# A fused attention and mixture-of-experts layer: work moved between VectorE and GpSimd, and a new order of the stage before attention

## What is computed

```python
xn = _layernorm(x, axis=-1)
queries, keys = xn @ w_q, xn @ w_k                    # 64 wide
scores = where(causal, queries @ keys.T * 64 ** -0.5, -inf)
attention = softmax(scores) @ (xn @ w_v1 @ w_v2)
logits = xn @ w_router.T                              # 16 experts
mask = one_hot(top_1(logits)); s = sigmoid(logits) * mask
gate, up = split((s.T[:, :, None] * xn) @ gate_up_proj)
expert_out = (up * silu(gate)) @ down_proj            # summed over experts
shared = (silu(xn @ w_gate.T) * (xn @ w_up.T)) @ w_down.T
moe = shared + expert_out
```

## Time and profile before

| | us |
|---|---|
| median of three runs | 242.66 (242.14 to 243.34) |
| the profiled execution | 243.21 |
| its span, first to last instruction | 239.9 |
| PE busy | 211.4 (88%) |
| PE weight loads busy | 183.3 (76%) |
| DVE busy | 155.7 (65%) |
| ACT busy | 130.6 (54%) |
| POOL busy | 110.8 (46%) |

### The profile page before, as it was taken

One profiled execution on the slowest core, in us unless ns is written; L12 is line 12 of the kernel. 1 busy time (PEld: TensorE's weight loads), 2 busy tenths in 40 slices (PEclk: granted clock), 3 DMA queues, 4 the chain that ended last, 5 costly groups with the idle time before them and its releaser, 6 DMA issues.

```text
span 239.9 us, 4858 instructions
## 1 busy us (share of the span) xinstructions
PE 211.4 (88%) x1399; PEld 183.3 (76%) x1401; DVE 155.7 (65%) x396; ACT 130.6 (54%) x329; POOL 110.8 (46%) x130
## 2 busy tenths in 40 slices
PE   4695999999996669999992899999999999899993
PEld 4484887898775559979881679998898897798792
DVE  3946887867748667678769466996665666405501
ACT  2354688678452566675674245554444444655741
POOL 1903030300001767777796006665665666738700
PEclk9997999999999999999998599999999999999999
DMA  6999999900000631541460113233233220019731
GB/s 174 398 361 337 190 172 303 256 23 0 0 4 1 176 99 55 146 132 48 103 172 0 47 44 87 78 85 80 85 84 87 81 77 19 3 45 290 237 87 44
DMA packets 30004, 28.26 MB, mean 118 GB/s; under 512 B 2563, under 2 KB 27146, under 8 KB 29344
## 3 DMA queue, kind: packets, MB, share of 16 engines
q1 hardware_dynamic: 27456, 23.77, 38.0%
q0 software_dynamic: 2528, 4.24, 5.6%
HBM read 14.28 MB, written 10.50 MB: 103 GB/s over the span
## 4 chain that ended last, share of the span: by engine, by line
PE 76%; DVE 12%; issue 5%; ACT 3%; DMA 1%; POOL 1%; DVEq 0%; ACTq 0%
PE acc L1163 13%; PE acc L1237 9%; PE big L1004 8%; PE big L1006 7%; PE big L1005 7%; PE mid L1147 6%; PE acc L1061 6%; PE mid L1226 4%; PE big L1134 4%; PE big L1131 4%; PE mid L1114 2%; DVE wel L732 2%; PE mid L1034 2%; PE acc L1025 1%; DVE stats L454 1%
## 5 line engine op out<-in xcount | busy, mean ns | idle before, releaser
L429 POOL DMA_INDIRECT y_rows<-y,ids x47 | 46.0, 978 | 36.7 <-ACT y L966 19.3
L419 POOL DMA_INDIRECT scratch<-rows,slot x32 | 32.3, 1009 | 41.3 <-DVE slot L651 30.7
L1163 PE MATMUL acc<-vr_all,pt 128*128 128x128 f32 x288 | 40.3, 277 | 0.6 <-ACT pt L912 0.3
L1163 PEld LDWEIGHTS acc<-vr_all,pt 128*128 128x128 f32 x288 | 36.5, 191 | 2.0 <-issue 1.1
L690 DVE TENSOR_REDUCE negmax<-big 128x1 f32<-128x128 f32 (+7 forms) x32 | 24.0, 755 | 21.2 <-PE big L1134 20.9
L905 ACT ACTIVATE prob<-big,negmax 128x128 f32<-128x128 f32 (+7 forms) x32 | 23.8, 744 | 19.6 <-DVE negmax L690 19.4
L912 ACT COPY pt<-mid 128x512 f32<-128x512 f32 (+3 forms) x48 | 22.8, 476 | 13.5 <-PE mid L1147 13.0
L774 DVE COPY eht<-mid 128x512 f32<-128x512 f32 (+1 forms) x24 | 16.3, 680 | 21.2 <-PE mid L1226 21.2
L966 ACT COPY y<-acc 128x256 f32<-128x256 f32 (+1 forms) x24 | 8.8, 368 | 34.0 <-PE acc L1237 34.0
L1237 PEld LDWEIGHTS acc<-wed,eht 128*128 128x128 f32 x188 | 24.5, 191 | 3.7 <-issue 1.9
L1147 PE MATMUL mid<-identf,prob 128*128 128x128 f32 x144 | 23.8, 274 | 3.3 <-ACT prob L905 2.7
(11 more groups left out here) (128 smaller groups left out, 439.2 us busy)
## 6 DMA issues: line engine op xcount, KB each, us to landing
we_raw<-w_gate_up SPq DMA_DIRECT2D x4, 1024.0 KB, 11.8
scratch<-blank SPq DMA_DIRECT2D x1, 3120.0 KB, 25.3
xe<-scratch SPq DMA_DIRECT2D x24, 130.0 KB
wed<-w_down SPq DMA_DIRECT2D x1, 2048.0 KB, 30.4
q_raw<-qk_all SPq DMA_DIRECT2D x8, 256.0 KB, 4.9
k_raw<-qk_all SPq DMA_DIRECT2D x8, 256.0 KB, 5.2
expert_out<-y_rows SPq DMA_DIRECT2D x8, 256.0 KB, 4.9
out<-res SPq DMA_DIRECT2D x8, 256.0 KB, 3.8
```

What stands on the lines that cost most here:

```text
L419: pool.indirect_dma_start(scratch, bass.IndirectOffsetOnAxis(ap=slot[:, t:t + 1], axis=0), rows[:, t, :], None).then_inc(row_sent[t % FLY] ...
L429: pool.indirect_dma_start(y_rows, bass.IndirectOffsetOnAxis(ap=ids[:, t:t + 1], axis=0), y[p % NY][:, t % 2, :], None, bounds_check=NT * P ...
L1163: last = pe.matmul(acc[g][:, cols], pt[n % 2][:, cols], v, start=kb == 0 and r == 0, stop=True, skip_group_check=True)
```

## The change

- *Start.* POOL's plain constants are filled ahead of the first `rsqrt`; its other constants wait for the first `xt_lo`. PE has 28 warm-up transposes where it had 12, and transposes group 1 only behind the first values product. DVE takes the statistics of batch 1 in one piece ahead of xt_lo(1).
- *Normalizing.* POOL normalizes groups 2 to 7, each behind its `rsqrt`; DVE keeps groups 0 and 1.
- *Low parts of the expert weights.* All sixteen go to POOL: experts 0 to 2 wait for xt_lo(3), 3 to 5 for xt_lo(4), 6 to 8 for xt_lo(6), 9 to 11 for xt_lo(7); experts 12 to 15 are made in eighths of 64 columns, one behind each indirect DMA of rows. ACT casts the high parts on a new schedule, the last two behind the exps of batch 0.
- *Split of keys and queries for batch 0.* Both halves move one step earlier: `split_k`, `split_q_lo` (0, 0) stand behind xt_lo(6), (0, 1) behind xt_lo(7), in both cases ahead of the next hidden(g - 2, 1).
- *Placing tokens.* `count` goes ahead of gate_up(7, 0), `rank` between the two halves of gate_up(7), `place_experts` and `place_tokens` between the `hidden` of group 6 and 7; down(6) and down(7) go behind scores of batch 0. `name_experts` moves to batch 1.
- *Scores.* The first four blocks of a batch lie in the four halves of the two PSUM tiles, so that they wait for fewer exps.
- *DMAs.* SP loads x ahead of the weights, and the last quarter of the weights, the blank table and the down weights behind the first load of queries and keys.

```diff
@@ sync
-            load_x(1)
-            for b in range(B):
-                if b >= 2:
-                    load_x(b)
...
+            load_x(1)
+            for b in range(B - 1):
+                if b < B - 2:
+                    load_x(b + 2)
+                load_weights(b)
...
             load_raw(0)
+            load_weights(B - 1)
+            sp.wait_ge(blanked, 3)
+            sp.dma_start(scratch.rearrange("(t p) r -> p t r", p=P),
+                         blank[:, None, :].to_broadcast([P, NS, ROW])).then_inc(scratch_blank, 16)
+            sp.dma_start(wed[:, :, :], w_down).then_inc(wed_loaded, 16)
@@ gpsimd
+            pool.wait_ge(xtl_ready[0], 1)
             pool.wait_ge(const_step, 6)
...
+            def weights_lo(e, part=0, parts=1):
+                cols = slice(part * 2 * FE // parts, (part + 1) * 2 * FE // parts)
                 pool.wait_ge(weh_ready, e + 1)
+                last = pool.tensor_tensor(flat(wel[:, e:e + 1, cols]), flat(we_raw[:, e:e + 1, cols]),
+                                          flat(weh[:, e:e + 1, cols]).bitcast(F32), ALU.subtract)
+                if part == parts - 1:
+                    last.then_inc(wel_ready, 1)
+
+            def normalize(g):
+                b, u = g // 2, g % 2
+                t0 = (2 * b + u) * GT
+                pool.wait_ge(rstd_ready, 2 * b + u + 1)
+                for t in range(GT):
+                    pool.tensor_scalar(flat(rows[:, bass.ds(t0 + t, 1), 0:P]), flat(res[:, bass.ds(t0 + t, 1), :]),
+                                      mean[:, u * GT + t:u * GT + t + 1], rstd[:, u * GT + t:u * GT + t + 1],
+                                      ALU.subtract, ALU.mult).then_inc(xn_ready[u], 1)
+
+            def weights_beside(g):
+
+                pool.wait_ge(xtl_ready[g % 2], g // 2 + 1)
+                n = IN_STAGE // 4
+                first = (g - GT + (g <= GT)) * n
+                for e in range(first, first + n):
+                    weights_lo(e)
 
             for b in range(1, B):
                 for u in range(2):
                     rsqrt(b, u)
+                    normalize(2 * b + u)
+                if b == B - 2:
+                    weights_beside(2 * B - 5)
+                    weights_beside(2 * B - 4)
+            weights_beside(2 * B - 2)
+            weights_beside(2 * B - 1)
...
                                         rows[:, t, :], None).then_inc(row_sent[t % FLY], 16)
-            for e in range(ON_DVE, NE):
-                weights_lo(e)
+                weights_lo(IN_STAGE + t // PARTS, t % PARTS, PARTS)
@@ vector
             xt_lo(0)
-            dve.wait_ge(const_made, CONSTS)
             dve.wait_ge(x_loaded[1], 16)
-            statistics(1, range(BT // 2))
+            statistics(1, range(BT))
+            for part in (statistics_2, statistics_3, statistics_4, statistics_5):
+                part(1)
             xt_lo(1)
...
-                if g + 1 < NG:
-                    normalize(g + 1)
...
-                    if g == NG - 2:
-                        split_k(0, 0)
                     hidden(g - 1, 0)
                     xt_lo(g + 1)
                     if g == NG - 2:
-                        split_q_lo(0, 0)
+                        split_k(0, 1)
+                        split_q_lo(0, 1)
...
+                    if g == NG - 3:
+                        split_k(0, 0)
+                        split_q_lo(0, 0)
...
+            for part in range(4):
+                choose(B - 1, part)
             sum_tiles(0)
+            sum_tiles(1)
             hidden(NG - 2, 0)
-            sum_tiles(1)
+            place_experts()
             hidden(NG - 2, 1)
+            place_tokens()
             to_score(NG - 1)
             hidden(NG - 1, 0)
-            place_experts()
             hidden(NG - 1, 1)
-            add_shared(NG - 2)
...
-                    for k in range(PER_BATCH if b < B - 1 else 0):
-                        weights_lo(PER_BATCH * (b - 1) + k)
+                if b == 1:
+                    name_experts()
@@ scalar
                 if first:
-                    for i in range(3):
+                    for i in range(GT):
                         exp(b, i)
...
                     exp(b, BT - 1)
+                    for e in range(HIGH_FROM[-1], NE):
+                        weights_hi(e)
@@ tensor
-            warm_up(12)
+            warm_up(28)
...
+            count()
             gate_up(NG - 1, 0)
-            count()
+            rank()
             gate_up(NG - 1, 1)
-            down(NG - 2)
-            rank()
...
-                    for i in range(GT):
+                    for i in range(GT + 1):
                         scores(b, i)
                         if i == 1:
-                            down(NG - 1)
-                    scores(b, GT)
+                            down(NG - 2)
+                    down(NG - 1)
                     pe.wait_ge(ranks_used, 1)
                     transposes(b, 0)
@@ constants
+PARTS = 8
+IN_STAGE = 12
+HIGH_FROM = (0, 3, 6, 9, 10, 12, 14)
+PROB_ORDER = (0, 1, 2, 7, 3, 4, 5, 6)
```

More of the change, by code:

```diff
@@ L141, in build @@
         wsl = sb("wsl", [P, DOWN0 - QK0], F32R)
+        xth_at = top[0]
         a, a_end = overlay(top[0], [(f"xth{n}", [P, GC], F32R) for n in range(XB)]
@@ L554, in _ @@
             xt_lo(0)
-            dve.wait_ge(const_made, CONSTS)
             dve.wait_ge(x_loaded[1], 16)
-            statistics(1, range(BT // 2))
+            statistics(1, range(BT))
+            for part in (statistics_2, statistics_3, statistics_4, statistics_5):
+                part(1)
             xt_lo(1)
             top_logit(0)
-            statistics(1, range(BT // 2, BT))
-            for part in (statistics_2, statistics_3, statistics_4, statistics_5):
-                part(1)
             hidden(0, 0)
+            to_score(0)
             top_logit(1)
-            normalize(2)
-            to_score(0)
+            dve.wait_ge(const_made, CONSTS)
             choose(0, 0)
             xt_lo(2)
+            choose(0, 1)
             hidden(0, 1)
             to_score(1)
-            choose(0, 1)
             dve.wait_ge(x_loaded[2], 16)
@@ L715, in first_half @@
                         if i == 1:
-                            place_tokens()
-                            split_k(0, 1)
-                            split_q_lo(0, 1)
-                        if i == 2:
+                            add_shared(NG - 3)
+                        if i == 4:
+                            add_shared(NG - 2)
                             add_shared(NG - 1)
@@ L853, in step @@
                 score_tanh(g)
-                for e in range(3 * (g - 2), min(3 * (g - 1), NE)):
+                for e in range(HIGH_FROM[g - 2], HIGH_FROM[g - 1]):
                     weights_hi(e)
-                if g == NG - 2:
+                if g == NG - 3:
                     split_q_hi(0, 0)
+                    split_q_hi(0, 1)
                 gate(g - 1, 0)
@@ L904, in exp @@
                 act.wait_ge(rden_ready, FIRST + b)
-                act.activation(prob[i][:, 0:(i + 1) * P], big[i % 2][:, 0:(i + 1) * P], ACT.Exp,
+                buf, at = score_block(i)
+                act.activation(prob[i][:, 0:(i + 1) * P], buf[:, at:at + (i + 1) * P], ACT.Exp,
                                bias=negmax[:, i:i + 1], accum_out=den[:, i:i + 1]).then_inc(exp_done, 1)
@@ L915, in first_half @@
                 if first:
-                    for i in range(3):
+                    for i in range(GT):
                         exp(b, i)
-                    for u in range(2):
-                        act.wait_ge(shared_added[u], FIRST + B)
-                    exp(b, 3)
                     keep_pt(b, 0)
@@ L1178, in first_half @@
                     scores(b, BT - 1)
+                if first:
+                    scores(b, GT + 1)
                 for n in range(GT):
-                    if first and n + 1 < GT:
-                        scores(b, GT + n + 1)
+                    if first and n < 2:
+                        scores(b, GT + n + 2)
+                    if first and n == GT - 1:
+                        weigh(b, n)
+                        transposes(b, n + 1)
+                        continue
                     if not (b == B - 2 and n == GT - 1):
```

84 lines of the change are left out of this document (37 added, 47 removed).

## The result

| | before | after |
|---|---|---|
| median | 242.73 (241.2 to 243.49, 7 runs) | 244.27 (243.41 to 245.86, 7 runs) |
| profiled execution, span | 243.21, 239.9 | 244.08, 242.3 |
| granted clock, mean | 0.977 | 0.961 |
| PE / DVE / ACT / POOL busy | 211.4 / 155.7 / 130.6 / 110.8 | 215.8 / 147.1 / 130.0 / 150.3 |

The ratio after to before is 1.0078, 95% interval [1.0039, 1.0116]: slower, by about 1.5 us, where +2.3 was forecast. Medians are of all executions of a kernel; a ratio is of the faster ones on both sides, those at most 1.5% above the fastest of their kernel. The sum hit for partly wrong reasons, and the profile shows which.

A forecast was written before the change was run, and what follows sets the result against it. PE was taken to bound the kernel, busy nine tenths of nearly every slice, so only its gaps could be won; the terms summed to +2.4 on 243.21, so 245.6, or 245.0 beside the median, own range 242 to 249.

The forecast's parts named there:

- Start: Kernel start up to group 2's transposes: normalizing on POOL at 0.3 us each lets PE go on earlier, -5.3 us.
- Normalize and first low parts: POOL's normalizes and experts 0 to 2 delay xt_lo and DVE's work in the projection stage, +1.0 us (0 to 4).
- Steps 6 and 7: Ahead of down(4) and down(5): POOL holds k_lo for three subtractions, so hidden comes late, +5.1 and +4.5 us.
- first rival: DVE gets in between two of POOL's subtractions, so k_lo and q_lo wait 1.25 us each; 240.8 us, chance 0.25.
- second rival: Nothing on DVE is held by POOL's subtractions, stalls 1.4 and 0.8 us, no clock loss; 233.3 us, chance 0.20.
- Clock: PE's granted clock falls behind two gaps of 5 us ahead of down(4) and down(5), 1.7 us each, +3.4 us.
- Behind step 7: From down(5) to the tokens' slots and batch 0's scores: the new order of placing tokens saves time, -2.1 us.
- Transfers: Row transfers with an eighth of a subtraction (0.25 us) behind each: rows late by 0 to 1.6, +0.5 us.
- third rival: Each eighth between row transfers pays a 0.3 us dispatch; 253 us on top of the forecast, chance 0.12.
- Start of the experts: DVE, free of its four subtractions, makes xel sooner; PE's gap falls from 5.1 to 1.75 us, -3.4 us.
- Clock given back: Behind the shorter gap at the experts' start, 1.3 of 2.1 us lost to low clock return, -1.3 us.

The follow-up runs named there:

- before_again: The kernel before, unchanged, executed and traced a second time; it took 239.31 us.
- after_again: The changed kernel, unchanged, run again on another chip, where the kernel before has a median of 285.5 us; 257.29 us (252.63 to 258.71).

## Why the prediction was right or wrong

The forecast (245.0) and its direction held; several of its terms did not, and their errors cancel. The mechanism that carried the sum, DVE held behind three of POOL's subtractions in each of steps 6 and 7, did not happen, so that the closeness of the total is luck.

- **Start, -5.3: wrong, measured -1.9.** The step that failed is the 0.3 us for a tensor_scalar on POOL, taken from a quarter of a subtraction and from a select. It is 0.79, outside the 0.2 to 0.6 kept for it. The gap stayed, and so did the half clock behind it (0.58 from 18 to 22 us), though the term had counted on full clock. With DVE's normalize project_x(2) comes 5.4 ahead of the trace of the prediction (18.68 beside 24.04), but 3.2 ahead of before_again (21.87), where no clock falls: the 1.4 that the term takes from the clock is there only against an execution in which it fell.
- **Normalize and first low parts, +1.0: measured +2.0**, inside its 0 to 4. It is the one wait of 2.19 for xtl(5), behind six of POOL's subtractions, since experts 3 to 5 came right behind 0 to 2.
- **Steps 6 and 7, +5.1 and +4.5: measured +2.6 and +2.9.** "Then POOL holds k_lo for 3 x 1.25" is the step that fell. k_lo and q_lo were held until the end of one subtraction each, 1.64 to 1.66; in step 6 k_lo even came in ahead of POOL (in after_again it was held there too, 1.65, and PE waited 3.54 instead of 2.63). That is the first rival's mechanism, at 1.25 each in the working and 0.95 measured. Its total of 240.8 shares the start term; with the measured -1.9 there it reads 244.2. The second rival (nothing held) fell with the first 1.64.
- **Clock, +3.4: measured +2.3**, all of it behind step 7 (down(5) 3.75 instead of 2.02 and the gate_up behind it); the gap of 2.63 in step 6 brought no fall. Where the clock falls changes from execution to execution: in after_again it falls behind the wait for xtl(5) (0.54 from 48 to 49 us) and behind neither of the two waits of 3.54.
- **Behind step 7, -2.1: right** (7.95 to 5.66, so -2.3). The slots came 10.7 after down(5) instead of 8.0, of which 2.3 are the clock above.
- **Transfers, +0.5: measured +1.3.** The period was right: 1.6 was assumed as the mean of before plus 0.25, and the mean of after is 1.58. Two misses offset each other in it, since a plain eighth takes 0.33 to 0.34, not 0.25, and the gap in front of a transfer falls from 0.30 to 0.17. The third rival (a dispatch for each eighth) fell: the idle time behind an eighth is less than that of before, not more.
- **Start of the experts, -3.4: right in kind, measured -4.7** (offset 6.9 to 2.2). Beside before_again, whose wait for xel is 1.8 shorter, it would be less.
- **Clock given back, -1.3: wrong, 0.** PE's gaps in front of the experts are now 1.27 and 0.92 instead of 5.12, and the clock is low for 6.8 us all the same (134.7 to 141.5). The term had taken the depth of the fall to follow the length of the single gap; these rows say it does not. In after_again the gaps are 2.67 and 0.79 and the clock is low for 3.4 us.

In sum -1.9 + 2.0 + 2.6 + 2.9 + 2.3 - 2.3 + 1.3 - 4.7 = +2.2, and 0.2 more up to the end make the measured +2.4 of the spans. The forecast had the start 3.4 us too good, normalize and first low parts 1.0, the transfers 0.8 and the giving back 1.3; it had the holding 4.1 too bad, its clock 1.1, the start of the experts 1.3 and the stretch behind step 7 0.2: 6.5 against 6.7. The spans are what the sum explains. The times of the two profiled executions differ by 0.9 only (243.21 and 244.08), since 3.3 us lie outside the span in the trace of before and 1.8 in that of after, and the medians differ by 1.5.

The Trainium skill ("SBUF — State Buffer", Who interferes with whom) says that the second of such a pair blocks until the first finishes. The 1.64 and 1.66 of after agree. I had set it aside for one row of 4.27, and the 2.47 of the second execution shows that row was no accident; but it was the minority case, and the rule gave the better term.

## What to carry to other kernels

Price an operation that moves to another engine by a row of that operation on that engine; a neighbour of the same shape was off by 2.6 times here, and 2.1 us of the gain of the first stage hung on it. When two engines exclude each other in SBUF, look for what stands behind the held instruction: with the two splits ahead of hidden PE waited 6.7 us for h, with them behind it 0.5, under the same holding (1.2 of it came back ahead of project_x(7) and 2.9 ahead of count). Take a second trace before a term is built on a fall of the clock: the same kernel, with the same wait of 2.4 us, had one at the start and did not have one. And a comparison on one chip can miss a loss of 30 us that another chip shows, so transfers that follow each other back to back on POOL deserve a second chip before they are called free.

## What the runs showed of the hardware

- tensor_scalar of 128x128 f32 with two pointer scalars: 0.79 us on POOL, 0.28 on DVE (1.12 for four).
- A held DVE subtraction of 512 columns: mostly 1.64 to 1.68 instead of 0.69, once 1.82 in each of two other kernels, and 2.47 and 4.27 in the kernel before; POOL's own was lengthened too, to at most 1.72 from 1.25. An instruction of eight columns beside it: 1.32 instead of 0.16. A cast of 512 columns with one SBUF input beside it: 1.04, 1.13 and 1.51 instead of 0.41.
- An indirect transfer mostly keeps POOL 0.96 to 0.98 us; 0.30 idle before the next if nothing is between, 0.33 of subtraction and 0.17 idle with an eighth. So an eighth costs 0.24 of period, not its own 0.33.
- The clock fell for about 6.8 us behind waits of 1.27 and 0.92 (after) as behind one of 5.12 (before), for 3.4 behind 2.67 and 0.79 (after_again), and did not fall behind one of 2.63. Behind PE's wait of 2.0 to 2.2 us for xtl(5) it fell in four traces and not in six.
